# A landing wait between GpSimd's pairs of indexed transfers in the last expert layer

## The chip, the cores and the metric

The kernel runs on one core of a Trainium2 chip. The metric is the device time of one execution in microseconds (us). Engines are called by the names of the profile: PE (TensorE matmuls), PEld (its weight loads), DVE (VectorE), ACT (ScalarE), POOL (GpSimd) and SP (SyncE, which here only issues DMAs).

## The reference, cut to what matters

A stack of four attention blocks and four feed-forward blocks on x of 32 x 128 x 128 float32, that is 4096 tokens of 128 numbers, in 32 tiles of 128 tokens. Only the last block is touched, a mixture of 8 experts with 2 experts for each token and a capacity for each expert:

```python
logits = x @ Wg.T
top_v, top_i = jax.lax.top_k(logits, K)                 # K = 2 of E = 8
gates = jax.nn.softmax(top_v, axis=-1)
pos = jnp.cumsum(onehot, axis=0) - 1                    # a token's place at its expert
keep = pos_f < cap
exp_batches = zeros((E, cap, d)).at[flat_e, pos_safe].set(x[tok], mode='drop')
h = jnp.einsum('ecd,edf->ecf', exp_batches, W1)
inp, gate = jnp.split(h, 2, axis=-1)
h = jax.nn.gelu(inp, approximate=False) * gate
exp_out = jnp.einsum('eci,eid->ecd', h, W2)
gathered = exp_out[flat_e, jnp.minimum(pos_safe, cap - 1)]
out = segment_sum(where(keep, gates_f, 0)[:, None] * gathered, tok)
x = x + out
```

## The kernel before, in words

The last expert layer is `capacity_ffn` (from L2217). Its tokens come in four chunks of 8 tiles (b = 0 to 31), and the chunks form three parts: part 0 is chunk 0, part 1 is chunks 1 and 2, part 2 is chunk 3 (`CAPACITY_PARTS`). For each chunk DVE works out to which row of the DRAM buffer `slots_in` each token goes (`locate`, L2493 writes `index`). For each tile POOL then issues two indexed transfers, one for each chosen expert, which write the 128 rows of the tile to `slots_in` (L2413, "scatter", 64 in all). All scatters of a part count up one semaphore, `scattered[p]`.

The rows of one expert are worked through in units of 256. There are 15 units in part 0 (u = 0 to 14), 23 in part 1 (15 to 37) and 15 in part 2 (38 to 52). For a unit SP loads the rows (L2355), PE turns them (L2767), ACT copies the result (L2675), PE multiplies with both halves of the first weights (L2781), ACT applies the GELU (L2681), DVE multiplies the halves (L2577), PE multiplies with the second weights (L2794), ACT copies the result (L2687) and SP stores it to `slots_out` (L2363). DVE also copies the weights of each unit into place (L2570). PE's order in step u is: first product of unit u+1, turning of unit u+2, second product of unit u. SP's order in step u is: load of unit u+5, then store of unit u. The load of a part's first unit waits for all scatters of that part (L2351), and what stands behind it on SP waits with it. So the load of unit 15 stands in SP's order just before the store of unit 10, and it needs the scatters of tiles 8 to 23.

When all units of a part are stored, POOL fetches the results back, again two indexed transfers for each tile (L2425, "gather", 64 in all), into a ring of 8 buffers; a tile past the eighth also waits until DVE has used the buffer (`x_added`). DVE adds the two gathered rows to x with their gates (`add_result`, L2582 and L2584). These additions stand at fixed places in DVE's order: tiles 0 and 1 in step 21, tiles 2 to 7 one in each of the steps 22 to 27; tiles 8 and 9 in step 40, tiles 10 to 22 one a step up to 52, all others after the last unit (`ADDS = {0: 21, 1: 40}`). DVE waits at that place if the gather hasn't landed, and the next units' DVE work is behind it.

POOL's own order in the layer is: small operations on the statistics, scatters of tiles 0 to 31, gathers of part 0, of part 1, of part 2. Everything is issued in that order by one engine. Before the change nothing waits between the transfers of a chunk, apart from the ring. An earlier expert layer (`routed_ffn`) gathers 16 tiles in pairs too (L1735), each pair behind a wait for the result of a unit.

Of the kernel before, what the change touches and what calls it, by code (L numbers as in the profile page):

```python
# [1502 lines left out]
def routed_ffn(nc, core, name, w1, w1_loaded, w2_dram, b1, router_w, norms, mix_w, mix_b_dram, b2_dram, slots_in, slots_out, late):  # L1503
# [22 lines left out]
    part_of_unit = [p for p, n in enumerate(unit_counts) for _ in range(n)]  # L1526
    LOWEST = -3.0e38
    g1, be1, g2, be2 = norms
    ctx = ExitStack()
    with ctx:  # L1530
# [228 lines left out]
        def _(dve):  # L1759
# [57 lines left out]
            def first_of_largest(c, k, left):  # L1817
                less = iota_less[:, None, :].to_broadcast([S, RT, NE])
                top = gates[:, k, chunk(c)]
                own.link(dve.tensor_reduce(top, left, AX.X, ALU.max))  # L1820
                own.link(dve.tensor_tensor(mark[:, :, :], left, over_e(top), ALU.is_equal))
                own.link(dve.tensor_tensor(mark[:, :, :], mark[:, :, :], less, ALU.mult))
                own.link(dve.tensor_reduce(best[:, :], mark[:, :, :], AX.X, ALU.min))
                own.link(dve.tensor_tensor(pick[:, k, chunk(c), :], less, over_e(best[:, :]), ALU.is_equal))

            def choose_first(c):
# [4 lines left out]
                first_of_largest(c, 0, pr[:, :, :])  # L1831
                own.link(dve.scalar_tensor_tensor(rest_p[:, :, :], pick[:, 0, chunk(c), :], LOWEST, pr[:, :, :],
                                                  ALU.mult, ALU.add))
# [387 lines left out]
def capacity_ffn(nc, core, name, w1, w1_loaded, w2_dram, router_w, capacity, slots_in, slots_out, out, front):  # L2221

    NE, FC = 8, w2_dram.shape[2]
    PARTS = CAPACITY_PARTS
    RT = 8
# [11 lines left out]
    FORWARD = 5  # L2237
    RING = 8
    SKIP = 100000.0
    LOWEST = -3.0e38  # L2240
    part_of_chunk = [p for p, (first, last) in enumerate(PARTS) for _ in range(first, last)]
    part_of_unit = [p for p, n in enumerate(unit_counts) for _ in range(n)]
    ctx = ExitStack()
    with ctx:
# [75 lines left out]
        scattered = [sem(f"scattered{i}") for i in range(len(PARTS))]  # L2320
# [11 lines left out]
        gathered = [sem(f"gathered{i}") for i in range(RING)]  # L2332
# [57 lines left out]
        @block.gpsimd  # L2390
        def _(pool):
            own = Steps(pool, pool_own)

            def inverse_root(c):
                at = chunk(c)
                pool.wait_ge(stats_done, c + 1)
                core.settle(pool)
                own.link(pool.tensor_scalar(rstd[:, at], mv[:, at, 1], LN_EPS, None, ALU.add))
                pool.tensor_tensor(rstd[:, at], rstd[:, at], core.minus_half[:, 0:RT], ALU.pow)\
                    .then_inc(rstd_done, 1)  # L2400

            def between(g):
                if g in (4, 6):
                    inverse_root(g // 2 - 2)

            layer.pool(pool, between)
            for c in range(NR):
                pool.wait_ge(index_done, c + 1)
                for b in range(c * RT, (c + 1) * RT):
                    if b in (2, RT):  # L2410
                        inverse_root(2 if b == 2 else 3)
                    for k in range(2):
                        pool.indirect_dma_start(  # L2413
                            out=slots_in[:, :], out_offset=bass.IndirectOffsetOnAxis(index[:, k, b:b + 1], 0),
                            in_=xn[:, b, :], in_offset=None, bounds_check=NE * NB * S - 1, oob_is_err=False)\
                            .then_inc(scattered[part_of_chunk[c]], 16)
            for p, (first, last) in enumerate(PARTS):
                pool.wait_ge(out_rows_done, p + 1)
                for i in range(BUF):
                    pool.wait_ge(y_stored[i], 16 * len(range(i, first_units[p + 1], BUF)))  # L2420
                for b in range(first * RT, last * RT):
                    if b >= RING:
                        pool.wait_ge(x_added, b - RING + 1)
                    for k in range(2):
                        pool.indirect_dma_start(  # L2425
                            out=yg[b % RING][:, k, :], out_offset=None, in_=slots_out[p][:, :],
                            in_offset=bass.IndirectOffsetOnAxis(index_out[:, k, b:b + 1], 0))\
                            .then_inc(gathered[b % RING], 16)

        @block.vector  # L2430
        def _(dve):
# [21 lines left out]
            def choose(c):  # L2453
# [5 lines left out]
                for k, left in enumerate((logits, rest_l[:, :, :])):  # L2459
# [8 lines left out]
                    if k == 0:  # L2468
                        own.link(dve.scalar_tensor_tensor(rest_l[:, :, :], picked, LOWEST, logits, ALU.mult, ALU.add))
                dve.tensor_tensor(chosen16[c % 2][:, 0:RT, :], pick[:, 0, chunk(c), :], pick[:, 1, chunk(c), :], ALU.add)\  # L2470
# [3 lines left out]
            def locate(c):  # L2474
# [10 lines left out]
                for what in range(2):  # L2485
# [6 lines left out]
                own.link(dve.tensor_scalar(over[:, :, chunk(c)], where[:, 0, :, :], float(capacity), None, ALU.is_ge))  # L2492
                dve.scalar_tensor_tensor(index[:, :, chunk(c)], over[:, :, chunk(c)], SKIP, where[:, 1, :, :],  # L2493
                                         ALU.mult, ALU.add).then_inc(index_done, 1)
# [319 lines left out]
def program(nc, ap, out, stages=range(8)):  # L2814
    core = Core()
    ctx = ExitStack()
    with ctx:
# [198 lines left out]
        if 7 in stages:  # L3016
            capacity_ffn(nc, core, "E3", exp3_w1, exp3_w1_loaded, ap["L3_exp_w2"], moe3_router, CAPACITY,
                         slots_in, slots_out, out,
                         lambda sb, sem, banks: OneHeadFront(core, sb, sem, banks, a3_w, a3_s))
# [96 lines left out]
```

## Time and profile before

| | |
|---|---|
| median of 3 runs | 1602.31 us (1596.95 to 1602.91) |
| span of the profiled execution | 1599.7 us |
| its own device time | not listed apart; the span is 2.6 us under the median |
| PE, DVE, POOL busy | 75%, 62%, 33% of the span |
| mean granted TensorE clock | 0.867 |
| indexed transfers | 256 in the kernel, of which 64 scatters (L2413) and 64 gathers (L2425) in this layer |
| last expert layer | the scatters start at 1270.6 us, the last gather at 1588.4 us |

The table is from the first part of the page, the view of the cores and the views of single lines. "Busy" is the time in which an engine executes; the granted clock is the share of full speed (2.4 GHz) that TensorE is allowed.

### The profile page before, as it was taken

What the parts mean: (1) busy time and instruction counts of PE and PEld (TensorE: products, weight loads), DVE (VectorE), ACT (ScalarE), POOL (GpSimd) and SP (SyncE); (2) the same over time, 40 slices, a digit from 0 to 9 for tenths busy, and PEclk for the clock granted to TensorE, in tenths of its full rate; (3) what the DMA queues carried; (4) which work ended last, traced back from release to release, by engine and by line L of the source; (5) the groups of instructions that cost most, each with busy time, mean ns of one, the idle gap of its engine ahead of it and who ended that gap; (6) DMA issues with size and microseconds to landing.
All of it is one profiled execution on the core that took longest, in us unless ns stands there. A gap on an engine that the chain in (4) does not pass through costs nothing. (4 is left out here: it accounts for less than half of the span.)

```text
span 1599.7 us, 34931 instructions
## 1 busy us (share of the span) xinstructions
PE 1204.2 (75%) x11141; PEld 938.0 (59%) x11154; DVE 991.3 (62%) x2920; ACT 674.5 (42%) x1429; POOL 535.6 (33%) x590
## 2 busy tenths in 40 slices
PE   2799974188779767799878799979996755369761
PEld 1577753177669635566644566756775644358661
DVE  3699876335424358989856799876786854244332
ACT  1467751055435313356545466753333413124330
POOL 2332303713535175444212433301111364330343
PEclk9999995589989858899989899998998857679976
DMA  7887622112223375545421866531003211123232
GB/s 178 203 214 190 180 71 105 43 54 62 70 75 107 81 164 151 132 112 133 132 48 33 182 166 160 146 93 39 0 0 119 75 61 62 49 76 102 88 96 66
DMA packets 138978, 164.58 MB, mean 103 GB/s; under 512 B 15308, under 2 KB 118754, under 8 KB 131728
## 3 DMA queue, kind: packets, MB, share of 16 engines
q1 hardware_dynamic: 130664, 146.62, 34.4%
q0 software_dynamic: 8192, 16.46, 3.7%
q8 instruction: 60, 0.98, 0.3%
q14 instruction: 62, 0.51, 0.1%
HBM read 111.98 MB, written 51.38 MB: 102 GB/s over the span
## 5 line engine op out<-in xcount | busy, mean ns | idle before, releaser
L586 DVE TENSOR_REDUCE A_neg_max<-A_s_bank 128x4 f32<-128x512 f32 x384 | 253.4, 688 | 49.7 <-PE A_s_bank L725 38.1
L448 ACT ACTIVATE A_probsT<-A_st_bank 128x512 f32<-128x512 f32 x384 | 222.4, 602 | 39.9 <-PE A_st_bank L738 37.3
L725 PE MATMUL A_s_bank<-A_k_stack,A_q_stack 72*128 72x128 bf16 x1536 | 158.3, 229 | 37.5 <-DVE A_neg_max L586 23.4
L738 PE MATMUL A_st_bank<-A_q_stack,A_k_stack 128*128 128x128 bf16 x1536 | 153.2, 224 | 7.0 <-DVE A_q_stack L602 6.2
L738 PEld LDWEIGHTS A_st_bank<-A_q_stack,A_k_stack 128*128 128x128 bf16 x1536 | 112.6, 103 | 52.2 <-issue 42.8
L725 PEld LDWEIGHTS A_s_bank<-A_k_stack,A_q_stack 72*128 72x128 bf16 x1536 | 106.9, 102 | 52.1 <-DVE A_neg_max L586 34.4
L752 PE MATMUL A_pv_bank<-A_probsT,A_v_pad 128*32 128x128 f32 x3072 | 128.1, 285 | 1.3 <-ACT A_probsT L448 0.9
L2052 ACT ACTIVATE E_h<-E_h_bank,w_L_b 128x256 f32<-128x256 f32 x184 | 76.7, 472 | 98.2 <-PE E_h_bank L2155 76.3
L2570 DVE COPY E_w_u<-exp_w 128x512 f32 x53 | 23.0, 436 | 150.2 <-DMA late_rows<-routed_out,late_index 89.3
L2425 POOL DMA_INDIRECT E_yg<-slots_out,E_index_out x64 | 60.6, 947 | 149.8 <-DMA slots_out<-E_ye 121.0
L2167 PE MATMUL E_y_bank<-E_w,E_h 128*128 x736 | 92.9, 280 | 12.4 <-DVE E_ye L1919 9.8
L2155 PE MATMUL E_h_bank<-E_xT,E_w_u 128*128 128x256 f32 x368 | 91.5, 394 | 8.1 <-issue 7.5
L2167 PEld LDWEIGHTS E_y_bank<-E_w,E_h 128*128 128x128 f32 x736 | 87.7, 195 | 15.3 <-issue 15.1
L2781 PE MATMUL E_h_bank<-E_xT,E_w_u 128*128 128x256 f32 x212 | 64.2, 431 | 40.5 <-ACT E_xT L2675 23.9
L2794 PE MATMUL E_y_bank<-E_w,E_h 128*128 x424 | 61.1, 290 | 39.3 <-issue 28.4
L752 PEld LDWEIGHTS A_pv_bank<-A_probsT,A_v_pad 128*32 128x32 f32 x3072 | 74.2, 111 | 24.8 <-ACT A_probsT L448 1.9
L461 ACT COPY A_outT<-A_pv_bank 128x512 f32<-128x512 f32 x99 | 58.0, 586 | 67.0 <-PE A_pv_bank L752 62.9
L1919 DVE TENSOR_TENSOR E_ye<-E_y_bank,E_b 128x256 f32<-128x256 f32 x46 | 19.5, 424 | 104.6 <-PE E_y_bank L2167 93.2
L2794 PEld LDWEIGHTS E_y_bank<-E_w,E_h 128*128 128x128 f32 x424 | 55.5, 204 | 41.5 <-issue 41.5
L1722 POOL DMA_INDIRECT routed_in<-E_r,E_index x64 | 62.8, 981 | 50.2 <-DVE E_index L1851 28.2
L2155 PEld LDWEIGHTS E_h_bank<-E_xT,E_w_u 128*128 128x128 f32 x368 | 69.2, 198 | 17.7 <-issue 8.3
L2413 POOL DMA_INDIRECT slots_in<-E_xn,E_index x64 | 63.1, 986 | 46.4 <-DVE E_index L2493 27.9
(372 smaller groups left out, 2670.4 us busy)
## 6 DMA issues: line engine op xcount, KB each, us to landing
A_q_stack<-q_scratch SPq DMA_DIRECT2D x48, 576.0 KB
A_k_stack<-k_scratch SPq DMA_DIRECT2D x32, 576.0 KB
q_scratch<-A_q_parts SPq DMA_DIRECT2D x48, 192.0 KB
A_k_stack<-k_scratch SPq DMA_DIRECT2D x48, 192.0 KB
E_xe<-slots_in SPq DMA_DIRECT2D x53, 128.0 KB
slots_out<-E_ye SPq DMA_DIRECT2D x53, 128.0 KB
A_ctxT<-in_ctxT SPq DMA_DIRECT2D x24, 256.0 KB
k_scratch<-A_k_parts SPq DMA_DIRECT2D x32, 192.0 KB
```

What stands on the lines that cost most here:

```text
L448: act.activation(probsT[n % 2][:, c * HQ:(c + 1) * HQ, :], st_bank[c % 2][:, :].rearrange("k (a q) -> k a q", a=HQ), ACT.Exp, scale=scale) ...
L586: dve.tensor_reduce(neg_max[:, c * HQ:(c + 1) * HQ], s_bank[c % 2][:, :].rearrange("q (a k) -> q a k", a=HQ), AX.X, ALU.max, negate=True). ...
L725: last = pe.matmul(s_bank[c % 2][:, a * S:(a + 1) * S], q_stack[slot][0:COMBO, h, at:at + S], k_stack[slot][0:COMBO, h, at:at + S], start= ...
L738: last = pe.matmul(dst, k_stack[slot][:, h, at:at + S], q_stack[slot][:, h, at:at + S], start=True, stop=spread)
L752: last = pe.matmul(pv_bank[a * VW:(a + 1) * VW, c * S:(c + 1) * S], v_pad[p][:, n % GB, h % vheads, :], probsT[n % 2][:, h, :], start=True ...
L1722: pool.indirect_dma_start(out=slots_in[:, :], out_offset=bass.IndirectOffsetOnAxis(index[:, k, b:b + 1], 0), in_=r[:, b, :], in_offset=Non ...
L2052: last = act.activation(h[u % 2][:, f, :], h_bank[(2 * u + q) % HB][:, f % 2 * UT:(f % 2 + 1) * UT], ACT.Silu, bias=b1[:, bass.ds(e * FC + ...
L2155: last = pe.matmul(dst, w1_u[u % 2][:, f * 128:(f + 1) * 128], xT[u % 3][:, :], start=True, stop=True)
L2167: last = pe.matmul(y_bank[:, j * D:(j + 1) * D], h[u % 2][:, f, j * S:(j + 1) * S], w2[:, bass.ds(e * (FC * D) + f * D, D)], start=(f == 0 ...
L2413: pool.indirect_dma_start(out=slots_in[:, :], out_offset=bass.IndirectOffsetOnAxis(index[:, k, b:b + 1], 0), in_=xn[:, b, :], in_offset=No ...
L2781: last = pe.matmul(bank[:, f * UT:(f + 1) * UT], w1_u[p][:, (c0 + f) * 128:(c0 + f + 1) * 128], xT[u % 3][:, :], start=True, stop=True)
L2794: last = pe.matmul(y_bank[:, j * D:(j + 1) * D], h[p][:, f, j * S:(j + 1) * S], w2[:, bass.ds(e * (FC * D) + f * D, D)], start=(f == 0), s ...
```

## The change

POOL waits before a tile's pair until all earlier scatters of the same part have landed, and before a gather pair until the pair of the tile before has landed. Chunk 0's scatters, the first pair of each part and the gathers of part 2 have no such wait. `PACE` is 1, so that every tile is paced.

```diff
+    PACE = 1
...
             layer.pool(pool, between)
+            sent = [0] * len(PARTS)
             for c in range(NR):
+                p = part_of_chunk[c]
                 pool.wait_ge(index_done, c + 1)
                 for b in range(c * RT, (c + 1) * RT):
                     if b in (2, RT):
                         inverse_root(2 if b == 2 else 3)
+                    if c >= 1 and sent[p] and b % PACE == 0:
+                        pool.wait_ge(scattered[p], 16 * sent[p])
                     for k in range(2):
                         pool.indirect_dma_start(
                             out=slots_in[:, :], out_offset=bass.IndirectOffsetOnAxis(index[:, k, b:b + 1], 0),
                             in_=xn[:, b, :], in_offset=None, bounds_check=NE * NB * S - 1, oob_is_err=False)\
-                            .then_inc(scattered[part_of_chunk[c]], 16)
+                            .then_inc(scattered[p], 16)
+                        sent[p] += 1
             for p, (first, last) in enumerate(PARTS):
                 pool.wait_ge(out_rows_done, p + 1)
                 for i in range(BUF):
                     pool.wait_ge(y_stored[i], 16 * len(range(i, first_units[p + 1], BUF)))
                 for b in range(first * RT, last * RT):
+                    if p + 1 < len(PARTS) and b > first * RT and b % PACE == 0:
+                        pool.wait_ge(gathered[(b - 1) % RING], 32 * ((b - 1) // RING + 1))
                     if b >= RING:
                         pool.wait_ge(x_added, b - RING + 1)
                     for k in range(2):
```

## Rows read from the trace of the kernel before

**Rows 1.** Busy time by stretch: start:end, length, engines, PEclk, DMA share, GB/s
```profile
1342.00:1382.00 40.00, 10.00 (x43) 7.93 (x41) 2.72 (x9) 1.96 (x5) 28.31 (x29) 0.64 0.18 57
...
1440.00:1501.00 61.00, 60.71 (x370) 55.01 (x371) 26.39 (x58) 27.83 (x64) 0.02 (x1) 0.95 0.32 100
1501.00:1533.00 32.00, 11.73 (x54) 9.65 (x52) 5.01 (x12) 3.89 (x10) 20.79 (x22) 0.70 0.26 71
```

**Rows 2.** Timeline of SP, stores of units 0, 4, 27 and 37: start, length
```profile
1326.95 0.33 SPq L2363 DMA_DIRECT2D slots_out<-E_ye  x1
...
1345.86 0.33 SPq L2363 DMA_DIRECT2D slots_out<-E_ye  x1
...
1470.07 0.32 SPq L2363 DMA_DIRECT2D slots_out<-E_ye  x1
...
1498.48 0.32 SPq L2363 DMA_DIRECT2D slots_out<-E_ye  x1
```

**Rows 3.** Timeline of all engines inside the scatter burst: start, length, [idle before]
```profile
1346.08 1.15 PE L2794 MATMUL E_y_bank<-E_w,E_h 128*128 x8 [1.40 <-issue]
...
1373.67 0.37 ACT L2687 COPY E_ye<-E_y_bank 128x256 f32<-128x256 f32 x1 [17.21 <-issue]
```

**Rows 4.** Busy time by stretch, the earlier expert layer's paced gathers
```profile
465.00:525.00 60.00, 59.57 (x415) 55.30 (x414) 24.96 (x73) 33.76 (x80) 29.73 (x32) 1.00 0.36 102
```

**Rows 5.** Timeline of POOL, two of the 16 pairs of that stretch
```profile
471.85 0.94 POOL L1735 DMA_INDIRECT late_rows<-routed_out,late_index  x1 [1.54 <-DVE E_ye L1919]
473.09 0.95 POOL L1735 DMA_INDIRECT late_rows<-routed_out,late_index  x1 [0.30 <-issue]
475.59 0.95 POOL L1735 DMA_INDIRECT late_rows<-routed_out,late_index  x1 [1.55 <-DVE E_ye L1919]
```

**Rows 6.** Timeline, a gather pair between two stores in the last layer
```profile
1541.75 0.32 SPq L2363 DMA_DIRECT2D slots_out<-E_ye  x1
...
1544.59 0.32 SPq L2363 DMA_DIRECT2D slots_out<-E_ye  x1
```
**Rows 7.** Timeline of POOL, the same place
```profile
1542.29 0.95 POOL L2425 DMA_INDIRECT E_yg<-slots_out,E_index_out  x1 [1.22 <-DVE x_sb L2584]
```

**Rows 8.** Timeline, landing of chunk 0's last scatter and SP's loads behind it
```profile
1292.06 0.97 POOL L2413 DMA_INDIRECT slots_in<-E_xn,E_index  x1 [0.30 <-issue]
```
**Rows 9.** Timeline of all engines: the loads that waited for it
```profile
1295.33 5.85 SPq L2355 DMA_DIRECT2D E_xe<-slots_in  x6
```

**Rows 10.** Timeline, POOL's start after the signal of DVE's index
```profile
1337.24 0.18 DVE L2493 SCALAR_TENSOR_TENSOR E_index<-E_over,E_where 128x16 uint32<-128x16 f32 x1
...
1338.21 1.05 POOL L2413 DMA_INDIRECT slots_in<-E_xn,E_index  x1 [17.60 <-DVE E_index L2493]
```

**Rows 11.** Timeline, a gather pair's second transfer and DVE's addition behind it
```profile
1570.92 0.95 POOL L2425 DMA_INDIRECT E_yg<-slots_out,E_index_out  x1 [0.30 <-issue]
...
1573.43 0.35 DVE L2582 SCALAR_TENSOR_TENSOR x_sb<-E_yg,E_gates,x_sb 128x128 f32<-128x128 f32 x1 [7.31 <-DMA E_yg<-slots_out,E_index_out]
```

**Rows 12.** Timeline, the same beside SP's loads and stores
```profile
1502.23 0.95 POOL L2425 DMA_INDIRECT E_yg<-slots_out,E_index_out  x1 [0.30 <-issue]
...
1505.07 0.35 DVE L2582 SCALAR_TENSOR_TENSOR x_sb<-E_yg,E_gates,x_sb 128x128 f32<-128x128 f32 x1 [1.05 <-DMA E_yg<-slots_out,E_index_out]
```

**Rows 13.** Timeline, DVE's signal to a gather of POOL
```profile
1533.71 0.35 DVE L2584 SCALAR_TENSOR_TENSOR x_sb<-E_yg,E_gates,x_sb 128x128 f32<-128x128 f32 x1
...
1534.33 0.94 POOL L2425 DMA_INDIRECT E_yg<-slots_out,E_index_out  x1 [6.14 <-DVE x_sb L2584]
```

**Rows 14.** Timeline of POOL: tile 8's first scatter, first gathers of parts 1 and 2
```profile
1300.19 1.19 POOL L2413 DMA_INDIRECT slots_in<-E_xn,E_index  x1
...
1500.98 0.95 POOL L2425 DMA_INDIRECT E_yg<-slots_out,E_index_out  x1 [64.54 <-DMA slots_out<-E_ye]
...
1569.67 0.95 POOL L2425 DMA_INDIRECT E_yg<-slots_out,E_index_out  x1 [18.73 <-DMA slots_out<-E_ye]
```

**Rows 15.** The chain that ended last, in order of time
```profile
1567.17 1.77 DMA slots_out<-E_ye
...
1588.42 2.36 DMA E_yg<-slots_out,E_index_out
```

## The prediction

> **What bounds the kernel now.** I read the busy time by stretch first, then the timeline inside the stretches that stood out, then the chain that ended last. Between 1440 and 1501 us POOL issues nothing and PE is busy 60.71 of 61 us: the units are bound by PE there [rows 1]. From the store of unit 27 to that of unit 37 they take (1498.48 - 1470.07) / 10 = 2.84 us each [rows 2]. While POOL issues its transfers without a break the picture turns: from 1342 to 1382 PE is busy 10.00 of 40 us, from 1501 to 1533 it is busy 11.73 of 32 us, at a granted clock of 0.64 and 0.70 [rows 1]. DMA is no cause by its volume, its share is 0.18 and 0.26, less than in the stretch where all runs well [rows 1]. What is late is the signal from PE to the others: the second product of a unit ends at 1346.08 + 1.15 = 1347.2, and the ACT copy that needs it starts at 1373.67, after 17.21 us that the trace can't name, with POOL issuing all the time [rows 3]. So each burst costs the units tens of microseconds, and the bursts, not PE, set this layer's length.
>
> The trace also shows pairs with a pause behind them. In the earlier expert layer 16 gather pairs start 475.59 - 471.85 = 3.74 us apart [rows 5], and PE is busy 59.57 of 60 us at clock 1.00 [rows 4]. In the last layer a pair starts at 1542.29 [rows 7], between two stores that are 2.84 us apart, full pace [rows 6]. A pair with a pause leaves the units alone; a long burst does not.
>
> **The change part by part.** It removes nothing and adds 44 waits: 22 before scatter pairs (tiles 9 to 23, 25 to 31) and 22 before gather pairs (tiles 1 to 7, 9 to 23). All of them are real waits, because a transfer follows the one before after 0.30 us [rows 8] and lands over 2 us after its start.
>
> *Period of a scatter pair, s.* Two issues up to the second start: 1.05 + 0.30 = 1.35 us [rows 8, 10]. Landing: chunk 0's last scatter starts at 1292.06 and SP's first load behind it at 1295.33 [rows 8, 9]; of that 3.27 us some 1.0 is SP's own work for a load (an estimate: six of them stand in 5.85 us, rows 9), so the scatter had landed after about 2.3 us. Restart: the index is written at 1337.24 + 0.18 = 1337.42 and POOL's transfer starts at 1338.21, 0.79 later [rows 10]. s = 1.35 + 2.3 + 0.79 = 4.4 us, against 2.56 without the wait. No row shows a landing wait before a scatter, so bounds: below, the restart of a gather, 1533.71 + 0.35 to 1534.33 = 0.27 [rows 13], gives 3.9; above, 0.33 more of landing (next term) gives 4.8. I take 4.4, since rows 10 are the same instruction behind a wait.
>
> *Period of a gather pair, g.* 0.95 + 0.30 = 1.25 to the second start, then 1573.43 - 1570.92 = 2.51 until the one who waits goes on [rows 11], and 0.27 of restart [rows 13]: g = 4.0. Bounds: the landing of 2.36 in the chain [rows 15] gives 3.9, and 1505.07 - 1502.23 = 2.84 beside SP's traffic [rows 12] gives 4.4. I take 4.0, as rows 7 stand beside such traffic without harm.
>
> *What it moves.* POOL's order is one chain, and it becomes the path. Tile 8's pair starts at 1300.19 as before [rows 14]. Fifteen periods later, at 1300.2 + 66.0 = 1366.2, tile 23's starts; tile 24 opens a new part, follows after two issues (2.6) at 1368.8, and tile 31 seven periods later at 1399.6. Two issues and the restart (3.3) bring the first gather at 1402.9. Is anything else later? Unit 4 was stored at 1345.86, 4.7 us a unit after unit 0 [rows 2]; freed of the first delay it may come some 7 us earlier, and unit 9 at about 1356. The load of unit 15 then waits on SP until tile 23 has landed, 1366.2 + 3.65 = 1369.9. Behind it on SP are the stores from unit 10 on, and PE waits at its turning: some 7 to 14 us of new idle time. From about 1373 the units go on, and unit 21 is reached near 1398.
>
> There DVE waits for tiles 0 and 1, gathered only from 1402.9. The last of part 0, tile 7, lands at 1402.9 + 7 x 4.0 + 1.25 + 2.51 = 1434.7; the additions take two of 0.35 [rows 13], so DVE is free at about 1435.5. Unit 28 is stored about 2.9 later, unit 37 nine units of 2.84 later: 1464.0. In the kernel before, part 1's first gather starts 1500.98 - 1498.48 = 2.5 after that store [rows 2, 14]: now at 1466.4, 34.6 earlier. Its 16 pairs then rule the rest of the units (tile 21 in step 51, tile 22 in step 52): fifteen periods, two issues and a restart are 60 + 2.5 + 0.7 = 63.2, so part 2's first gather starts at 1529.6. Before it was 1569.67 [rows 14]. The tail behind it has no new wait and stays.
>
> The sum: 1529.6 - 1569.7 = -40.1 us on a span of 1599.7, that is 1559.6. The span is 2.6 under the median of the runs, so 1602.3 - 40.1 = 1562 is the number to compare. PE's saved stalls are worth more, but what was hidden by them, POOL's time, is what is late next. Each microsecond of s and each of g costs 22 us. At the low ends (3.9 and 3.9) the sum is 1549, at the high ends (4.8 and 4.4) 1580. The other edits (a counter, the name p) cost nothing at run time; the chunk 0 scatters and part 2's gathers are issued as before.
>
> A landing beside SP's traffic is seen 0.33 us later than one without [rows 11, 12]; if all 44 were, the sum would be 1562 + 44 x 0.33 = 1577. The Trainium skill (DMA: Bandwidth & Descriptors, "Queues, rings and completion order") has a rule that speaks against this change: a DMA's semaphore write lands only after every earlier write of that DMA engine, whichever queue it came from. The trace agrees with it in sign at most.
>
> **The rivals.** (a) *Slower: the landing that POOL now waits for is held up by SP's transfers in flight.* One store alone takes 1.77 us to land [rows 15]. If every one of the 44 landings came 1.77 later, the chain would be 78 us longer, 1562 + 78 = 1640. It decides from 40.1 / 44 = 0.91 us on each landing. For it: SP moves a load and a store for every unit, all through POOL's paced time. Against: rows 12 show 0.33, a fifth of it. The page named above would make this the rule. Chance 0.11.
>
> (b) *PE's signals stay late beside pairs.* From 1501 to 1533 PE lost 32 - 11.7 = 20 us over 22 transfers, 0.9 each [rows 1]. If that holds for paced ones, units 38 to 52 would need 15 x 2.84 + 32 x 0.9 = 71 us instead of 63, and the step from the wait of unit 15 on and at unit 28 a few us: +8 to +20, 1570 to 1582. Rows 4 to 7 speak against it, but those scatters had no paced example. Chance 0.17.
>
> (c) *A wash.* Landings at 2.84 or later and the restart of 0.79 at the gathers too: 22 x 0.4 + 22 x (0.33 + 0.52) = 28 more, 1590, and with 0.1 more on each landing 1594, no change. Chance 0.07.
>
> That the waits do nothing can't be, as the counts include every transfer sent; that they pass early neither.
>
> **How the numbers follow.** The forecast, units undisturbed and POOL's chain the path, has a chance of 0.65: 1562, own range 1549 to 1580. With (b) that is 0.82 for faster. Of (c) nearly all is put at no change, within 8 us (0.5%, about what a measurement of this kernel can tell from none), and 0.01 at faster: faster 0.83, same 0.06, slower 0.11. The range from 1546 to 1588 holds the forecast and (b), with the lower end a little under the sum at the low ends.
>
> **What would show it.** In the profile after: scatter pairs of tiles 9 to 31 about 4.4 us apart and gather pairs of parts 0 and 1 about 4.0 (right), 5 or more (rival a). ACT's copies follow PE's second products within about 1 us, and the long idle times without a name before L2687 are gone; if 3 us and more remain beside pairs, it is (b). A wait of SP at L2351 for scatters that was not there before, until about 1370. DVE waiting for gathers at L2582 in steps 21 to 27. First gather of part 1 near 1466, of part 2 near 1530. If PE still stands idle for 10 us and more while POOL is paced, the reading of the bursts is wrong.

## Result and profile after

The change makes the kernel faster: 1561.95 us, median of four runs (1556.9 to 1569.33), against 1602.61 for the kernel before beside it (four runs, 1596.95 to 1604.64). The ratio is 0.9765, 95% interval 0.974 to 0.9789. The profiled execution is the slowest of the four, 1569.33 us with a span of 1567.4, so its span is 32.3 us under that of before and the medians are 40.7 apart. Of this difference 5.3 us arise before any added wait: tile 8's pair starts at 1305.51 where it was at 1300.19 [rows 14].

The added waits, in POOL's timeline after: two pairs of scatters, the step from the last scatter to the first gathers, and two firsts of a part.

```profile
1305.51 1.19 POOL L2418 DMA_INDIRECT slots_in<-E_xn,E_index  x1
1307.01 1.03 POOL L2418 DMA_INDIRECT slots_in<-E_xn,E_index  x1 [0.30 <-issue]
1310.09 0.97 POOL L2418 DMA_INDIRECT slots_in<-E_xn,E_index  x1 [2.05 <-DMA slots_in<-E_xn,E_index]
...
1371.66 0.97 POOL L2418 DMA_INDIRECT slots_in<-E_xn,E_index  x1 [1.99 <-DMA slots_in<-E_xn,E_index]
...
1405.47 0.97 POOL L2418 DMA_INDIRECT slots_in<-E_xn,E_index  x1 [2.36 <-DMA slots_in<-E_xn,E_index]
1406.75 0.97 POOL L2418 DMA_INDIRECT slots_in<-E_xn,E_index  x1 [0.30 <-issue]
1408.03 1.00 POOL L2433 DMA_INDIRECT E_yg<-slots_out,E_index_out  x1 [0.30 <-issue]
...
1437.31 0.95 POOL L2433 DMA_INDIRECT E_yg<-slots_out,E_index_out  x1 [1.93 <-DMA E_yg<-slots_out,E_index_out]
...
1473.17 0.95 POOL L2433 DMA_INDIRECT E_yg<-slots_out,E_index_out  x1 [33.48 <-DMA slots_out<-E_ye]
...
1534.95 0.95 POOL L2433 DMA_INDIRECT E_yg<-slots_out,E_index_out  x1 [1.79 <-DMA E_yg<-slots_out,E_index_out]
...
1537.45 0.94 POOL L2433 DMA_INDIRECT E_yg<-slots_out,E_index_out  x1 [0.30 <-issue]
```

In brackets stands how long POOL was idle before the instruction and for what. Behind each landing wait there are some 2 us, and a scatter pair takes (1371.66 - 1305.51) / 15 = 4.41 us, a gather pair (1437.31 - 1408.03) / 7 = 4.18 in part 0 and (1534.95 - 1473.17) / 15 = 4.12 in part 1.

What it buys is in the busy time by stretch: start:end, length, PE, PEld, DVE, ACT, POOL busy, granted clock, DMA share, GB/s. The first stretch is that of the burst in [rows 1].

```profile
1342.00:1382.00 40.00, 26.23 (x143) 22.82 (x142) 19.93 (x72) 10.74 (x24) 18.70 (x19) 0.84 0.25 80
1440.00:1470.00 30.00, 29.19 (x187) 26.40 (x187) 11.57 (x24) 13.43 (x30) 0.00 (x0) 1.00 0.31 96
1473.00:1537.00 64.00, 44.61 (x241) 38.06 (x239) 23.43 (x55) 17.83 (x40) 30.55 (x32) 0.89 0.32 96
```

From 1342 to 1382 PE now works 26.23 us where it worked 10.00, at a granted clock of 0.84 for 0.64 [rows 1]. Beside part 1's gathers it is busy 44.61 of 64 us; there the adds of DVE follow gathers 4.1 us apart, and the units follow DVE.

The waits by engine from 1255 us on (us in total, times, longest):

```profile
DVE x_sb L2590 <- DMA E_yg<-slots_out,E_index_out: 69.8, 32, 5.3
POOL slots_in L2418 <- DMA slots_in<-E_xn,E_index: 47.2, 22, 2.7
POOL E_yg L2433 <- DMA E_yg<-slots_out,E_index_out: 42.0, 22, 2.4
ACT E_ye L2695 <- DMA late_rows<-routed_out,late_index: 2.4, 1, 2.4
```

The two POOL lines are the 44 waits. The last line needs a word, as the experiments are read by it. The view names what it takes for the release of a wait; before some waits it names late_rows, a tile of an earlier layer that was gathered long before and can't be what was waited for. Where such a name stands before an ACT copy or a DVE copy, the thing late is PE's signal (as in [rows 3], where it is called issue). Such waits sum to 2.4 us here. In the kernel before, the same view has:

```profile
DVE E_w_u L2570 <- DMA late_rows<-routed_out,late_index: 89.3, 7, 29.2
ACT E_xT L2675 <- DMA late_rows<-routed_out,late_index: 27.3, 6, 8.7
ACT E_act_h L2681 <- DMA late_rows<-routed_out,late_index: 23.9, 6, 8.7
```

The engines wait beside each other, so these are not added up, and a wait is not the lateness of its signal: DVE stood idle for up to 29.2 us, and part of that lay before PE's product was done. How late the signals are can be read by pairing them in the trace, for each unit the end of PE's product with the start of the ACT or DVE instruction that needs it (four a unit, 208 in all, as the DVE copies of units 0, 1, 15 and 38 wait for something else). In the kernel before, 25 of these start over 1 us after everything that they needed, the latest of them 23.3 us; the product of [rows 3] ends 26.4 us before ACT goes on (1373.67 - 1347.23), a part of which ACT spends on another such wait. In the changed kernel one is over 1 us late, by 1.9 us: PE's product ends at 1409.36 and ACT's copy starts at 1411.24, right beside the four transfers from 1405.47 to 1409.33 that have no wait between them.

That PE itself is in time is seen beside [rows 3], between the product's end at 1347.2 and ACT's start at 1373.67:

```profile
1356.10 0.37 ACT L2675 COPY E_xT<-E_t_bank 128x256 f32<-128x256 f32 x1 [5.79 <-DMA late_rows<-routed_out,late_index]
1356.52 2.08 PE L2781 MATMUL E_h_bank<-E_xT,E_w_u 128*128 128x256 f32 x4 [9.29 <-ACT E_xT L2675]
```

PE goes on 0.05 us after ACT's copy has ended (1356.10 + 0.37), with POOL issuing, and is at a later product while the signal of the earlier one is still out. So signals from PE are late in the burst, those to PE are not.

SP's timeline after: the stores of units 0 and 9, the load of unit 15 and the stores of units 27 and 37.

```profile
1322.14 0.33 SPq L2364 DMA_DIRECT2D slots_out<-E_ye  x1
...
1357.05 0.33 SPq L2364 DMA_DIRECT2D slots_out<-E_ye  x1
...
1376.20 0.34 SPq L2356 DMA_DIRECT2D E_xe<-slots_in  x1
...
1441.19 0.32 SPq L2364 DMA_DIRECT2D slots_out<-E_ye  x1
...
1470.67 0.32 SPq L2364 DMA_DIRECT2D slots_out<-E_ye  x1
```

Unit 37 is stored at 1470.67, 27.8 us before its old time [rows 2], though unit 15's load had to wait for the scatters until 1376.20.

### The profile page after: what moved, and what is told of

The parts are those of the page before. It is cut to its first block and busy times, and to the rows that moved or that the text cites. A ratio compares the mean times of both kernels' runs of the same rounds, so it can differ in the third digit from the quotient of the medians.

```text
span 1567.4 us, 34947 instructions
## 1 busy us (share of the span) xinstructions
PE 1202.4 (77%) x11141; PEld 936.1 (60%) x11154; DVE 990.7 (63%) x2920; ACT 675.1 (43%) x1429; POOL 537.0 (34%) x590
## 5 line engine op out<-in xcount | busy, mean ns | idle before, releaser
L2155 PE MATMUL E_h_bank<-E_xT,E_w_u 128*128 128x256 f32 x368 | 93.1, 399 | 9.4 <-issue 8.7
L310 POOL TENSOR_TENSOR A_split_r<-A_k_f,A_k_parts 128x512 f32<-128x512 f32 (+1 forms) x21 | 26.1, 1242 | 152.5 <-ACT A_k_parts L472 77.0
L767 PE MATMUL A_t_bank<-ident,A_outT 128*128 128x128 f32 x396 | 66.8, 293 | 7.7 <-ACT A_outT L461 6.0
```

What stands on the lines that cost most here:

```text
L767: last = pe.transpose(t_bank[:, a * S:(a + 1) * S], outT[:, a, :], core.ident[:, :])
L2155: last = pe.matmul(dst, w1_u[u % 2][:, f * 128:(f + 1) * 128], xT[u % 3][:, :], start=True, stop=True)
```

## Experiments

Three causes could carry the gain, and the runs take them apart: (1) POOL's unbroken runs of indexed transfers make PE's signals late, and any break mends it; (2) transfers in flight must land before more are sent; (3) only one of the two bursts matters. A further question is what is late next: POOL's chain, or DVE's adds that stand too early among the units. Each ratio is to the kernel before on the same chip.

### One kind of wait alone

Scatters wait, gathers do not:

```diff
-                    if p + 1 < len(PARTS) and b > first * RT and b % PACE == 0:
-                        pool.wait_ge(gathered[(b - 1) % RING], 32 * ((b - 1) // RING + 1))
```

> Only the 22 waits before scatter pairs stay; the gathers are issued without a break as before. Theory (long unbroken runs of POOL's transfers hold up PE's signals, pairs with a pause don't; POOL's chain is then the path): scatters 4.4 us a tile, PE undisturbed until about 1403, then a stall of some 17 us beside the burst of part 0's gathers and one of some 25 us beside part 1's; 1575 us (1568 to 1582). Rival (all of the gain comes from the gathers, and the scatter waits only lengthen POOL's chain): 1602 or more.

Gathers wait, scatters do not:

```diff
-                    if c >= 1 and sent[p] and b % PACE == 0:
-                        pool.wait_ge(scattered[p], 16 * sent[p])
```

> Only the 22 waits before gather pairs stay; the scatters are issued as before. Theory: the layer runs as in the kernel before up to unit 16 (stalls of PE in the scatter bursts, 10 of 40 us busy), then no stall; unit 37 stored about 1479, part 2's first gather near 1546, 1579 us (1572 to 1586). Rival (all of the gain comes from the scatters): 1602. Rival (either set alone gives the whole gain, as the other's stalls are covered by POOL's chain): 1562 for both.

Measured: scatter waits alone 1576.09 us, ratio 0.9853 (0.9804 to 0.9902); gather waits alone 1580.61, ratio 0.9887 (0.9836 to 0.9938). With the kernel before at 1600.93 that is 24.8 and 20.3 us, both inside the range expected. Both bursts matter; the two gains add up to 45.1 us, a little more than the 40.7 of both together, which is less than the intervals can tell apart. (3) falls. Of the 208 paired signals 12 are over 1 us late in either kernel. With scatter waits alone the timeline (all engines) shows a stall in part 0's burst of gathers:

```profile
1410.79 0.38 PE L2773 MATMUL E_t_bank<-ident,E_xe 128*128 128x128 f32 x2
...
1422.55 0.37 ACT L2681 COPY E_xT<-E_t_bank 128x256 f32<-128x256 f32 x1 [8.74 <-DMA late_rows<-routed_out,late_index]
```

PE turned the unit by 1410.79 + 0.38 = 1411.17, and ACT's copy of it starts 11.4 us later. With gather waits alone the scatter burst keeps its stall, two stores that follow each other:

```profile
1344.92 0.33 SPq L2364 DMA_DIRECT2D slots_out<-E_ye  x1
...
1373.14 0.33 SPq L2364 DMA_DIRECT2D slots_out<-E_ye  x1
```

### Breaks without a landing

Both waits are replaced by a short operation of POOL on a tile of its own, of two lengths:

```diff
-                        pool.wait_ge(scattered[p], 16 * sent[p])
+                        pause()
...
-                        pool.wait_ge(gathered[(b - 1) % RING], 32 * ((b - 1) // RING + 1))
+                        pause()
```

pause() is one tensor_tensor with pow in the long form (1.7 us), one tensor_scalar in the short form (0.3 us).

> Each of the 44 landing waits is replaced by one small POOL operation of about 1.7 us (a power on 128x8), so POOL stops issuing for some 1.9 us without waiting for anything. Theory (a pause in the issuing is enough): 1562 us, within 8. Rival (it is the wait for the landing that frees PE's signals): stalls of 10 us and more come back in PE, 1590 to 1620.

> The same with one POOL operation of about 0.25 us, so a tile's pair takes about 2.9 us, and the next pair starts before the last has landed. If any break lets PE's signals through, POOL's chain is 22 x 1.5 + 22 x 1.3 = 62 us shorter and the units bound: 1515 to 1530 us. If what counts is that few transfers are in flight or that the pause is long enough, the stalls are back and it is 1590 to 1605 us, as before the change.

Measured, long: 1579.63 us, ratio 0.9877 (0.9811 to 0.9942). POOL's timeline:

```profile
1314.84 1.04 POOL L2423 DMA_INDIRECT slots_in<-E_xn,E_index  x1 [0.81 <-POOL E_pause_of L2409]
1316.19 0.97 POOL L2423 DMA_INDIRECT slots_in<-E_xn,E_index  x1 [0.30 <-issue]
1317.18 1.68 POOL L2409 TENSOR_TENSOR E_pause_of<-E_pause_of,minus_half 128x8 f32<-128x8 f32 x1
1319.66 1.03 POOL L2423 DMA_INDIRECT slots_in<-E_xn,E_index  x1 [0.81 <-POOL E_pause_of L2409]
```

A scatter pair takes 1319.66 - 1314.84 = 4.82 us, 0.41 more than with the wait, and POOL's chain is the path, so 22 such pairs alone cost 9 us; the gather periods are longer too (4.3 us). The time lies 17.6 us above the one expected and outside its 8 us. POOL's chain has most of it: from tile 8's pair to part 2's first gather it takes 1545.35 - 1300.19 = 245.2 us, 13.2 more than in the changed kernel, 10.1 of them up to the first gather. The other 4 us are not traced, and there are only two runs. But no wait with the name late_rows is left in its layer, and none of the 208 signals is over 1 us late: PE's signals are prompt without any landing wait.

Measured, short: 1549.47 us, ratio 0.9688 (0.9625 to 0.9751), lower than with the landing waits, though on two runs and with intervals that just meet (0.9751 and 0.974), and between the two numbers expected. Its POOL timeline, scatters and then gathers:

```profile
1310.99 0.27 POOL L2409 TENSOR_SCALAR E_pause_of<-E_pause_of 128x8 f32<-128x8 f32 x1
1312.06 1.02 POOL L2423 DMA_INDIRECT slots_in<-E_xn,E_index  x1 [0.79 <-issue]
1313.38 0.98 POOL L2423 DMA_INDIRECT slots_in<-E_xn,E_index  x1 [0.30 <-issue]
...
1381.98 0.28 POOL L2409 TENSOR_SCALAR E_pause_of<-E_pause_of 128x8 f32<-128x8 f32 x1
1382.53 1.01 POOL L2438 DMA_INDIRECT E_yg<-slots_out,E_index_out  x1 [0.27 <-issue]
```

The same operation makes a break (from the end of one transfer's issue to the next, the operation in it) of 1.07 us (1310.99 to 1312.06) between scatters and of 0.55 (1381.98 to 1382.53) between gathers, since the restart is 0.79 in one case and 0.27 in the other. And the signals tell the two apart: from 1290 to 1375, beside scatters, no wait has the name late_rows; from 1379 to 1402, beside gathers, they are these:

```profile
DVE E_w_u L2583 <- DMA late_rows<-routed_out,late_index: 13.5, 2, 7.6
ACT E_ye L2700 <- DMA late_rows<-routed_out,late_index: 9.4, 3, 3.9
```

By pairs, one signal is late by 1.5 us beside the scatters, and 25 more in this kernel are late by 1.2 to 5.3 us, all beside gathers. This speaks against (2), if weakly: a scatter pair starts every 3.4 us, a little before the last one has landed (the second start 1.3 us after the first, and 2.3 of landing, make 3.6), and the units run on. The last run of the next section has transfers in flight all the time and settles it. What remains is (1), with a question of how much break is enough.

### Fewer breaks, other breaks

Landing waits at every second tile only:

```diff
-    PACE = 1
+    PACE = 2
```

> The landing waits only at every second tile, so POOL issues four transfers and then lets them land. A pair of tiles then takes 2.84 + 4.4 = 7.2 us in place of 8.8 (scatters) and 8.3 (gathers), 3.6 per tile. Theory (what delays PE's signals is POOL's unbroken run; in the burst of the kernel before the first late signal comes some 4.5 us after its start with scatters, and in the third transfer with gathers): scatters of four cost the units next to nothing, gathers of four make PE's signals late by 1 to 3 us each time; time 1548 (1538 to 1560). Rival, only the length of POOL's chain counts: 22 x 0.8 + 22 x 0.55 = 30 us less, 1532 or below. Rival, a run of four is already as bad as a burst: 1575 or above.

Measured: 1535.91 us, ratio 0.9646 (0.961 to 0.9682), a little under the range expected for late signals and above what the chain alone would give. The runs are now four transfers long, three steps of 1.27 us and 0.97, some 4.8 us in all, with a break of 2.06 (POOL's timeline):

```profile
1304.89 0.97 POOL L2418 DMA_INDIRECT slots_in<-E_xn,E_index  x1 [2.06 <-DMA slots_in<-E_xn,E_index]
...
1308.72 0.97 POOL L2418 DMA_INDIRECT slots_in<-E_xn,E_index  x1 [0.30 <-issue]
1311.76 0.97 POOL L2418 DMA_INDIRECT slots_in<-E_xn,E_index  x1 [2.06 <-DMA slots_in<-E_xn,E_index]
```

Its waits from 1295 to 1375, beside the scatters:

```profile
DVE E_w_u L2578 <- DMA late_rows<-routed_out,late_index: 5.5, 1, 5.5
ACT E_act_h L2689 <- DMA late_rows<-routed_out,late_index: 4.7, 3, 3.2
```

The share of time that the breaks take is 2.06 / 6.87 = 0.30 here and 1.07 / 3.4 = 0.31 with the short operation, yet here signals are late and there only one is (by pairs, 19 over 1 us late in this kernel, the latest 4.7 us). The length of an unbroken run counts, not the share alone. It is the one comparison that tells the two apart, and its breaks differ also in kind, a landing wait here and an operation there.

One short operation between scatter tiles, and n between gather tiles, or one after every single transfer of the gathers:

```diff
-                        pool.wait_ge(scattered[p], 16 * sent[p])
+                        pause(1)
...
-                        pool.wait_ge(gathered[(b - 1) % RING], 32 * ((b - 1) // RING + 1))
+                        pause(n)
```

and, for the last of the three,

```diff
                             .then_inc(gathered[b % RING], 16)
+                        if k == 0 and p + 1 < len(PARTS):
+                            pause(1)
```

> No landing waits: one short POOL operation between tiles of scatters, three in a row between tiles of gathers (about 1.1 us in which POOL issues no transfer, as the scatters of the short pause have it). Theory (a quiet of about 1.1 us for each pair lets PE's signals through, whichever the direction, and 0.55 us does not): gathers take 3.4 us a tile, no signal of PE is late by over 1 us beside them, unit 37 is stored by 1450, and the time is 1535 (1526 to 1545). Rival, gathers need their landing (the direction matters, not the quiet): signals late by 2 to 7 us as with the short pause, 1547 to 1560.

> Scatters with one short POOL operation between tiles, gathers with two. In the run with three, POOL issued nothing for 1.36 us between two pairs of gathers (1382.58 to 1383.94) and a tile took 3.6 us; in the run with one, some 0.55 us and 2.84 us, with PE's signals late. With two: about 1.05 us, 3.3 us a tile. Theory, about 1.1 us of quiet suffices: no late signals, part 1's gathers 16 x 0.3 = 5 us shorter than with three and part 0's end 2.4 us sooner: 1525 (1518 to 1531). Rival, the quiet that is needed lies above 1.1 us with gathers: signals late again, 1535 to 1545.

> The same sum of quiet as with two operations (about 1.1 us for each tile of gathers), but cut in two: one short operation after every single transfer, so that no two transfers follow each other directly and no quiet is longer than 0.55 us; a tile takes 3.1 us. Theory A, what counts is the length of one unbroken run of issuing: a run is now 1 us and PE's signals are prompt, time as with two operations or below, 1520 to 1528. Theory B, what counts is one quiet of about 1 us in which waiting signals get through: signals late as with the single short operation, 1540 to 1555.

| gathers | break between runs, us | transfers in a run | signals over 1 us late, of 208 (latest, us) | time, us | ratio (95%) |
|---|---|---|---|---|---|
| one operation a pair | 0.55 | 2 | 26 (5.3) | 1549.47 | 0.9688 (0.9625 to 0.9751) |
| two a pair | 1.00 | 2 | 2 (1.6) | 1522.63 | 0.9544 (0.9517 to 0.957) |
| three a pair | 1.36 | 2 | 2 (1.6) | 1530.27 | 0.9608 (0.9575 to 0.9641) |
| one after each transfer | 0.52 | 1 | 0 | 1522.43 | 0.9521 (0.9493 to 0.9549) |

The last three came out as their theories expected. Both late signals of the kernel with three stand beside tile 31's scatters and tile 0's gathers, four transfers from 1374.20 on that no break parts there either.

The breaks with two and with one after each transfer, POOL's timeline of either kernel:

```profile
1446.57 0.56 POOL L2410 TENSOR_SCALAR E_pause_of<-E_pause_of 128x8 f32<-128x8 f32 x2
1447.57 1.00 POOL L2439 DMA_INDIRECT E_yg<-slots_out,E_index_out  x1 [0.44 <-POOL E_pause_of L2410]
```

```profile
1446.06 0.25 POOL L2410 TENSOR_SCALAR E_pause_of<-E_pause_of 128x8 f32<-128x8 f32 x1
1446.58 1.01 POOL L2439 DMA_INDIRECT E_yg<-slots_out,E_index_out  x1 [0.27 <-issue]
```

The waits with the name late_rows: a single one of 1.8 us with two operations, none with three, none with one after each transfer. The last is the sharpest test: the same 0.5 us of break that left DVE waiting for up to 7.6 us after runs of two does no harm after runs of one. It does raise the share of the breaks, from 0.55 / 2.84 = 0.19 to (2 x 0.52) / 3.2 = 0.33, so by itself it doesn't part the length of a run from the share; the kernel with runs of four does. From 1379 to 1405, all of it beside part 0's gathers, its busy time is

```profile
1379.00:1405.00 26.00, 25.75 (x160) 22.81 (x159) 13.55 (x31) 11.48 (x26) 21.25 (x32) 1.00 0.46 135
```

PE 25.75 of 26 us at clock 1.00, with POOL busy 21.25 us. With the single operation a pair, the same stretch has PE at 16.24 of 26 us and at 0.74 (both kernels' first gathers start near 1380, 1379.69 there):

```profile
1379.00:1405.00 26.00, 16.24 (x72) 12.99 (x71) 6.57 (x16) 5.04 (x13) 18.23 (x24) 0.74 0.28 83
```

Theory B of that run, that a waiting signal needs one quiet of about 1 us, falls. And so does (2): the gathers here start some 1.6 us apart, while a landing takes 2.4 us or more, so there are always transfers in flight. These two kernels beat both the kernel before and the changed one by more than the intervals.

### Are the adds too early?

```diff
-    ADDS = {0: 21, 1: 40}
+    ADDS = {0: 27, 1: 43}
```

> All waits kept; DVE's adds of part 0's and part 1's tiles are placed some steps later among the units (27 and 43 in place of 21 and 40), so that each tile has been gathered when its add comes. Theory: with the pairs paced, the adds are due before their gathers and DVE's waits hold the units back; with the adds later unit 37 is stored some 12 us sooner (after: 1470.7), part 1's first gather moves with it, and the time is 1550 (1544 to 1556). Rival: the units are not held back by the adds (PE has other things to do, or the table of part 2 comes later anyway): 1562 within 5. Second rival: adds pushed to the end lengthen the tail: over 1567.

> Scatters with one short POOL operation in place of the landing wait (3.42 us a tile, units undisturbed in the run of the short pause), gathers with the landing waits (4.15 a tile, no late signals), and DVE's adds later (27 and 43). Theory: the scatters end 22 x 1.0 = 22 us sooner than in the changed kernel, units start as before and stay free of late signals, and the adds no longer hold them: 1562 - 22 - 5 = 1535 (1528 to 1545). Rival, the units (PE) are now the bound and neither the shorter chain of scatters nor the later adds give all of it: 1547 to 1556, like the short pause alone.

Measured: 1552.81 us, ratio 0.9742 (0.9715 to 0.9769), all landing waits kept. In its trace tile 8's pair starts at 1298.27 and unit 37 is stored at 1451.74, 153.5 us later; in the changed kernel these are 1470.67 - 1305.51 = 165.2 us apart. So the adds did hold the units, by 11.7 us. Part 2's first gather comes 1519.65 - 1298.27 = 221.4 us after tile 8's pair, 10.5 sooner than the 231.9 of the changed kernel. The time is inside the range expected, but the step is not separable in it: the interval overlaps with 0.974 to 0.9789. With the short operation for the scatters as well (landing waits only at the gathers) it is 1536.1, ratio 0.9636 (0.9602 to 0.9669), as expected.

On the faster kernels the adds were set three steps and one step later (24 and 41):

> The kernel with one and three short operations (1530 us), and DVE's adds set three steps later for part 0 (24 for 21) and one for part 1 (41 for 40). Theory: DVE still waits 51 us in all for gathers and holds the units back in part 0, so unit 37 is stored some 4 to 6 us sooner: 1525 (1519 to 1529). Rival: with the shorter gathers the units are held by PE itself, and the adds' place is worth nothing: 1530 within 3.

> The kernel with a short POOL operation after every transfer of the gathers (1522.4 us), and DVE's adds set later (24 and 41). Theory: as between the two kernels with one and three operations (1530.3 and 1525.4), about 5 us less: 1518 (1513 to 1522). Rival: the gathers are shorter here than there (3.2 against 3.6 us a tile) and arrive in time for the adds, so that their place is worth nothing: 1522 within 3.

Measured: 1525.37, ratio 0.958 (0.9533 to 0.9628), against 0.9608 without; and 1524.17, ratio 0.9542 (0.9512 to 0.9573), against 0.9521 without. The first is as expected but within the intervals, the second went to the rival: where gathers come 3.2 us apart, the place of the adds is worth nothing that can be measured.

## Why the prediction was right

It was right in sign, size and mechanism. Set against tile 8's pair, which no added wait precedes, the steps of the sum come out as follows (us after the start of that pair):

| step | predicted | measured |
|---|---|---|
| tile 23's scatters start | 66.0 | 66.2 |
| tile 31's | 99.4 | 100.0 |
| first gather | 102.7 | 102.5 |
| part 0's last gather pair starts | 130.7 | 131.8 |
| unit 37 stored | 163.8 | 165.2 |
| part 1's first gather | 166.2 | 167.7 |
| part 2's first gather | 229.4 | 231.9 |

- **The scatter period** was built from a landing of 2.3 and a restart of 0.79 us, seen elsewhere in the trace; 4.4 expected, 4.41 measured. The idle time of 2.05 behind the second issue holds both.
- **The gather period** was 0.12 to 0.18 too short, as it used the landing beside no traffic; the rows beside SP's traffic [rows 12] would have given 4.4, too long by 0.2 to 0.3. Over 22 waits the shortfall is some 3 us, more than the whole of the sum's error of 2.5. Against it went the restart of 0.7 that was priced twice where a part's last pair is followed by the next gather: there is none, only the 0.30 that stands between any two transfers.
- **The new wait at unit 15.** SP's load goes at 1376.20, and PE's turning waits 10.3 us (7 to 14 expected). By its letter this meets the last sign of the prediction, that 10 us of idle PE beside a paced POOL would refute the reading of the bursts. It doesn't: the wait is one for SP's load, which the prediction had priced, and PE's next longest is 6.8 us, for DVE at 1418.
- **DVE's wait for gathers** from step 21 on came as told: from 1408 to 1450 eight waits, 20.4 us. The run with later adds shows that it cost the units 11.7 us, which the sum held without naming it as a price.
- **The tail** stayed: 1567.4 - 1537.45 = 30.0 us from part 2's first gather to the end, 1599.7 - 1569.67 = 30.0 before.
- **The equality of the medians** (1562.0 told, 1561.95 measured) is partly luck. The runs spread over 12 us, and the profiled one begins this layer 5.3 us later than the one that the sum was made against: its span of 1567.4 is 7.8 above the 1559.6 told, 5.3 from that and 2.5 from the sum.

Rival (a), landings held up by SP's transfers in flight, asked for 1.77 us on each landing. The landings themselves stand in the chain that ended last, here the first and the longest of part 0:

```profile
1409.33 2.48 DMA E_yg<-slots_out,E_index_out
...
1417.23 3.10 DMA E_yg<-slots_out,E_index_out
```

The 22 that POOL waits for took 2.40 to 3.10 us, 2.63 on average, against 2.36 without such traffic in [rows 15], and 2.51 up to the instruction that goes on in [rows 11]: 0.1 to 0.3 of delay on average and some 0.7 at most. The Trainium skill (DMA: Bandwidth & Descriptors, "Queues, rings and completion order") holds that a semaphore write comes only after every earlier write of that DMA engine, from any queue. With SP's loads and stores running through all of it, no more than that is seen of it here. Rival (b), signals late beside pairs, is refuted for the paced kernel (one late signal, of 1.9 us) but its thought was sound: with breaks of 0.55 us it comes true. Rival (c) needed 0.4 and 0.85 us more a pair; it was 0.01 for the scatters and 0.12 to 0.18 for the gathers.

What the prediction did not see is that the landing was not the point. It spoke of a pause, but priced none shorter than a landing; one short operation between scatter pairs and one after each gather do better by (0.9765 - 0.9521) x 1597 = 39 us.

## What to carry to other kernels

Look at what the other engines lose while GpSimd issues indexed transfers back to back, before asking what the transfers cost themselves: here the cure was not fewer transfers but gaps between them. Cheap gaps do, and a short operation on GpSimd makes them without tying its chain to a landing; take the shortest that leaves no late signal in the waits. And when a burst is stretched, go through everything that was placed by the burst's old timing (here DVE's adds).

## What was not expected of the hardware

- In an unbroken run of GpSimd's indexed transfers signals that PE sends are late, by up to 23 us in the kernel before: every wait with the name late_rows stands before an ACT or a DVE instruction. Signals to PE are not: from unit 3 on, in the kernel before and the changed one, each of its first and second products starts within 0.3 us of the last thing that it needed. In the stall shown above PE's product ended at 1411.17 and ACT went on at 1422.55, with the DMA engines far from full in such stretches (0.18 and 0.26 in [rows 1]). By which path the transfers hold up PE's signals, no run here tells.
- Runs of two transfers (2.3 us) leave the units alone with a break of 1.00 us between gathers and 1.07 between scatters, and 0.55 between gathers is too short; runs of one do with 0.52; after runs of four (4.8 us) even 2.06 us leave single signals up to 4.7 us late. Where exactly the bounds lie, and whether they hold for other sizes of transfer, was not tried. How a landing wait and an operation of the same length compare at equal period was not tried either.
- The restart behind an operation is 0.79 us before a scatter and 0.27 before a gather. The cause is open.
